# Graph attention with residual norm: pass sums weighted by shares from GpSimd, mask units kept in pairs, moments and normalising spread

## What is computed

```python
xt  = einsum('ni,hio->hno', x, W)                    # 4 heads of 64
src = einsum('hnf,hf->hn', xt, a[:, :64]);  dst = einsum('hnf,hf->hn', xt, a[:, 64:])
e   = leaky_relu(src[:, :, None] + dst[:, None, :], 0.2)
e   = where(adj > 0, e, -inf)
h   = einsum('hij,hjf->hif', softmax(e, axis=2), xt)   # heads side by side: 256 columns
out = layernorm(x + h)                               # over the 256 columns, eps 1e-5
```

## Time and profile before

| | before |
|---|---|
| median of 3 runs | 2212.24 us (2212.24 to 2214.11) |
| profiled execution | 2213.66 us |
| its span | 2212.1 us |
| PE matmul busy | 2108.5 us, 95% |
| DVE busy | 2069.6 us, 94% |
| ACT busy | 2011.0 us, 91% |
| GpSimd busy | 89.6 us, 4% |
| chain that ended last | PE 51%, DVE 21%, ACT 10%, issue 9% |

### The profile page before, as it was taken

The page is one execution under the profiler, slowest core; times in us unless marked ns, Lnnn a source line. Parts: engine busy times, 40 slices in busy tenths (PEclk is TensorE's granted clock), DMA queues, the critical chain, the costliest instruction groups (busy, mean ns, idle before and its releaser), DMA issues.

```text
span 2212.1 us, 79064 instructions
## 1 busy us (share of the span) xinstructions
PE 2108.5 (95%) x34304; PEld 2056.8 (93%) x34304; DVE 2069.6 (94%) x2288; ACT 2011.0 (91%) x2053; POOL 89.6 (4%) x88
## 2 busy tenths in 40 slices
PE   8768999999999999999999999999999999999996
PEld 4658999999999999999999999999999999999996
DVE  3899999999999999999999999999999999997775
ACT  3466998999999999999999999999999999999995
POOL 0110000010000100010000100010000100000000
PEclk9989999999999999999999999999999999999998
DMA  9699777766766676666766676666766677532310
GB/s 315 223 349 380 266 246 246 238 213 212 250 213 217 208 248 206 216 212 214 249 212 212 208 231 224 216 211 212 250 212 216 203 233 239 164 83 84 96 46 20
DMA packets 236441, 469.64 MB, mean 212 GB/s; under 512 B 14704, under 2 KB 22896, under 8 KB 236080
## 3 DMA queue, kind: packets, MB, share of 16 engines
q1 hardware_dynamic: 231600, 447.53, 61.8%
q0 software_dynamic: 4352, 16.78, 2.1%
q10 hardware_dynamic: 128, 0.13, 0.0%
HBM read 438.83 MB, written 25.56 MB: 210 GB/s over the span
## 4 chain that ended last, share of the span: by engine, by line
PE 51%; DVE 21%; ACT 10%; issue 9%; DMA 1%; DVEq 1%; POOL 0%; ACTq 0%; SPq 0%; POOLq 0%
PE acc L835 48%; ACT big L433 9%; DVE big L623 7%; DVE big L630 6%; PE tp L801 3%; DVE nat L539 2%; DVE big L615 1%; DVE stats L676 1%; ACT big L477 1%; DVE AT L553 1%; DVE big L637 1%; DVE nat L537 1%; DMA raw<-in_adj_dram 0%; DMA v_parts<-big 0%; DVE big L645 0%
## 5 line engine op out<-in xcount | busy, mean ns | idle before, releaser
L433 ACT ACTIVATE big<-big,d_all 128x1024 int8<-128x1024 f32 x1792 | 1896.5, 1141 | 84.0 <-PE acc L835 84.0
L835 PE MATMUL acc<-big 128*128 128x130 f16 x32768 | 1911.8, 220 | 30.4 <-DVE big L637 28.8
L835 PEld LDWEIGHTS acc<-big 128*128 128x128 fp8e5 x32768 | 1888.2, 98 | 39.7 <-issue 37.2
L623 DVE SCALAR_TENSOR_TENSOR big<-big,AT 128x1024 uint32<-128x1024 uint32 x512 | 627.2, 1225 | 62.1 <-ACT big L433 60.6
L630 DVE SCALAR_TENSOR_TENSOR big<-AT,big 128x1024 uint32<-128x1024 uint32 x512 | 626.7, 1224 | 4.3
L801 PE MATMUL tp<-ident,nat 128*128 128x128 f32 x1024 | 158.5, 278 | 41.9 <-DVE nat L537 33.0
L615 DVE TENSOR_SCALAR big<-big,d_all 128x1024 uint8<-128x1024 f32 x256 | 193.2, 755 | 0.0
L537 DVE TENSOR_SCALAR nat<-raw 128x2048 fp8e4<-128x2048 int32 x128 | 176.3, 1380 | 3.8 <-DMA raw<-in_adj_dram 3.8
L539 DVE TENSOR_SCALAR nat<-raw 128x2048 uint8<-128x2048 int32 x128 | 178.1, 1391 | 0.0
L553 DVE SCALAR_TENSOR_TENSOR AT<-AT,tp 128x512 uint32<-128x512 uint32 x224 | 154.8, 691 | 1.5
L801 PEld LDWEIGHTS tp<-ident,nat 128*128 128x128 f32 x1024 | 108.9, 142 | 49.2 <-DVE nat L537 38.8
(11 more groups left out here) (50 smaller groups left out, 377.9 us busy)
## 6 DMA issues: line engine op xcount, KB each, us to landing
raw<-in_adj_dram SPq DMA_DIRECT2D x256, 1024.0 KB, 5.7
big<-v_parts SPq DMA_DIRECT2D x512, 260.0 KB, 3.7
v_parts<-big SPq DMA_DIRECT2D x16, 1040.0 KB, 5.2
big<-s_rows SPq DMA_DIRECT2D x32, 512.0 KB, 5.5
AT<-in_x_dram SPq DMA_DIRECT2D x16, 512.0 KB, 6.5
big<-in_x_dram POOLq DMA_DIRECT2D x8, 1024.0 KB, 7.5
out_dram<-big POOLq DMA_DIRECT2D x8, 1024.0 KB, 9.0
big<-in_L_gnn_W_dram SPq DMA_DIRECT2D x2, 128.0 KB, 2.5
```

What stands on the lines that cost most here:

```text
L433: return nc.scalar.activation(sgn[:, g % NB, b, :], srow[:, h % 2, :], ACT.Sign, bias=dflat[:, r:r + 1], scale=-1.0)
L623: nc.vector.scalar_tensor_tensor(out=word(sgn, g % NB), in0=word(sgn, g % NB), scalar=EDGE[plane], in1=edges(g), op0=ALU.bitwise_and, op1= ...
L835: return nc.tensor.matmul(acc[:, k, o:o + 2 * VO], m[:, g % NB, b, t * P:(t + 1) * P], Vr[:, v:v + 2 * VO], start=opens, stop=False, skip_ ...
```

## The change

- **Shares.** GpSimd takes the two denominators of `u` times `ab` (`wden`, 128x16), adds them (`den`), and after DVE's reciprocal (`inverse`, after group 4) multiplies `ab` by it (`share`, 128x16). DVE multiplies `u` without its last column by `share` (`weigh`, after group 6) and adds both halves to `y` directly (`add_pos` after group 8, `add_neg` after group 9). `join` and `divide` go. For the last pass all of it is on DVE.
- **Pairs.** In steady chunks two units are kept by one instruction of 128x1024 (`keep_pair`) in steps 4j+3; it waits for the transposes of both, the second of which PE does at step 4j+2. `tp` is addressed as one tile of two banks, each unit's blocks in every second place. While chunk 0 runs, its own units are still kept alone, chunk 1's in pairs at steps 16+3j+2.
- **Moments and normalising.** Moments of tiles 0 to 2 after groups 10, 12, 14 of head 0, tiles 3 to 7 after groups 10 to 14 of head 1, `spread` after group 15 of head 1. ACT normalises tiles 0 to 5 in groups 5, 9, 13 of heads 2 and 3 and tiles 6 and 7 in groups 5 and 9 of the next chunk's head 0; in the last chunk, all 8 of the chunk before in groups 3, 7, 11, 15 of heads 2 and 3.
- GpSimd's program is unrolled, and ACT's loop starts one chunk later.

```diff
--- before.py
+++ after.py
...
@@ -248,13 +255,18 @@
         SIGNS_WITH = {9: 0, 11: 1, 13: 2, 15: 3}
-        def kept_at(first, after_first, s):
+        def kept_alone(first, s):
+            return made_at(True, s - 2) if first and 2 <= s < NG + 2 else []
+        def kept_pair(first, s):
             if first:
-                return [k for z in range(max(0, s - 2), s - 1) for k in made_at(True, z)]
-            if s < 3:
-                return [k - UN for z in range(s + 4 * NG - (2 if after_first else 3), s + 4 * NG - (1 if after_first else 2))
-                        if z < 4 * NG for k in made_at(after_first, z)]
-            return made_at(False, s - 3)
+                return [(s - NG) // 3] if s >= NG and (s - NG) % 3 == 2 else []
+            return [s // 4] if s % 4 == 3 else []
+        def sums4():
+            return u.rearrange("p (t c) v -> p t c v", c=2)
         @block.sync
...
@@ -380,19 +392,33 @@
             load_res(0, 0)
             load_res(1, 1)
-            def chunk(c, n):
-                deviation(c)
-                store(c, n)
-                pool.wait_ge(out_done, 16 * c + 16)
-                load_res(c + 2, n)
-            with pool.Fori(0, NC // 2 - 1) as i:
-                chunk(2 * i, 0)
-                chunk(2 * i + 1, 1)
-            for c in (NC - 2, NC - 1):
-                deviation(c)
-                store(c, c % 2)
+            def shares(p):
+                w = ab[:, p // H * T:(p // H + 1) * T, p % H, :]
+                pool.wait_ge(u_done, 3 * p + 6)
+                nc.gpsimd.tensor_tensor(out=wden[:, :, :], in0=sums4()[:, :, :, O], in1=w, op=ALU.mult).then_inc(wden_done, 1)
+                pool.wait_ge(wden_done, p + 1)
+                nc.gpsimd.tensor_tensor(out=den[:, :], in0=wden[:, :, 0], in1=wden[:, :, 1], op=ALU.add).then_inc(den_done, 1)
+                pool.wait_ge(rden_done, p + 1)
+                nc.gpsimd.tensor_tensor(out=share[:, :, :], in0=w, in1=rden[:, :].unsqueeze(2).broadcast_to([P, T, 2]),
+                                        op=ALU.mult).then_inc(share_done, 1)
+            for c in range(NC):
+                if c:
+                    shares(c * H - 1)
+                if c > 1:
+                    store(c - 2, c % 2)
+                    pool.wait_ge(out_done, 16 * (c - 1))
+                    load_res(c, c % 2)
+                shares(c * H)
+                if c:
+                    deviation(c - 1)
+                shares(c * H + 1)
+                shares(c * H + 2)
+            store(NC - 2, (NC - 2) % 2)
+            deviation(NC - 1)
+            store(NC - 1, (NC - 1) % 2)
             pool.wait_ge(out_done, 16 * NC)
...
                                          scale=rstd[:, t:t + 1]).then_inc(norm_done, 1)
-            def chunk(c, n, first=False):
+            def normalised_at(h, g, last):
+                if last:
+                    return [h % 2 * 4 + g // 4] if h >= 2 and g % 4 == 3 else []
+                return [(h - 2) * 3 + g // 4 - 1] if h >= 2 and g in (5, 9, 13) else []
+            def chunk(c, n, first=False, second=False, last=False):
                 for h in range(H):
                     p = c * H + h
                     act.wait_ge(row_in[h % 2], 32 * c + 16 * (h // 2 + 1))
...
@@ -489,14 +522,18 @@
                                 ins.then_inc(sgn_done, 1)
                             if g == 2 and b < 3 and not (first and h == 0):
                                 low(p - 1, b)
-                        if h == 1 and g >= 8 and not first:
-                            normalise(c - 1, 1 - n, (g - 8,))
+                        if h == 0 and g in (5, 9) and not first and not second:
+                            normalise(c - 2, n, (6 + g // 8,))
+                        if not first:
+                            normalise(c - 1, 1 - n, normalised_at(h, g, last))
             chunk(0, 0, first=True)
-            with act.Fori(0, NC // 2 - 1) as i:
+            chunk(1, 1, second=True)
+            with act.Fori(1, NC // 2 - 1) as i:
+                chunk(2 * i, 0)
                 chunk(2 * i + 1, 1)
-                chunk(2 * i + 2, 0)
-            chunk(NC - 1, 1)
+            chunk(NC - 2, 0)
+            chunk(NC - 1, 1, last=True)
             for part in range(3):
                 low(NP - 1, part)
             normalise(NC - 1, (NC - 1) % 2, range(T))
...
@@ -538,20 +575,21 @@
                 else:
                     nc.vector.tensor_scalar(to, of, 0.0, 59.0, ALU.is_gt, ALU.add).then_inc(conv_done, 1)
-            def keep(k, u, plane, fresh=False, n=0, g=0):
+            def keep(k):
                 dve.wait_ge(tp_done, k + 3)
-                if not fresh:
-                    z = (g - u // 2) % NG
-                    dve.wait_ge(pos_done if z == 0 else neg_done, n + 1 if z == 0 else n - z + 5)
-                to = AT[:, u // 2, :, u % 2, :]
-                of = tp[:, u % 2, :].bitcast(u32).rearrange("p (b i) -> p b i", b=B)
-                if fresh:
-                    nc.vector.tensor_scalar(to, of, EDGE[0], None, ALU.bitwise_and).then_inc(at_done, 1)
-                else:
-                    nc.vector.scalar_tensor_tensor(out=to, in0=to, scalar=EDGE[1 - plane], in1=of,
-                                                   op0=ALU.bitwise_and, op1=ALU.bitwise_or).then_inc(at_done, 1)
+                nc.vector.tensor_scalar(AT[:, k // 2, :, k % 2, :], tp[:, k % 2, :].bitcast(u32).rearrange("p (b i) -> p b i", b=B),
+                                        EDGE[0], None, ALU.bitwise_and).then_inc(at_done, 1)
+            def keep_pair(k, j, plane, n, g):
+                dve.wait_ge(tp_done, k + 4)
+                z = (g - j) % NG
+                dve.wait_ge(pos_done if z == 0 else neg_done, n + 1 if z == 0 else n - z + 5)
+                nc.vector.scalar_tensor_tensor(out=edges(j), in0=edges(j), scalar=EDGE[plane], in1=pair.bitcast(u32),
+                                               op0=ALU.bitwise_and, op1=ALU.bitwise_or).then_inc(at_done, 2)
             for g in range(NG):
                 dve.wait_ge(thin_done, g + 1)
...
@@ -637,38 +675,29 @@
                     ins = nc.vector.tensor_tensor(out=u_piece(piece), in0=u_piece(piece), in1=acc_piece(piece, 0), op=ALU.add)
                 ins.then_inc(u_done, 1)
-            def weigh(p, ec, eh):
-                dve.wait_ge(u_done, 3 * p + 6)
-                w = ab[:, bass.ds(ec * T, T), eh, :]
-                u4 = u.rearrange("p (t c) v -> p t c v", c=2)
-                nc.vector.tensor_tensor(out=u4, in0=u4, in1=w.unsqueeze(3).broadcast_to([P, T, 2, VO]),
+            def inverse(p):
+                dve.wait_ge(den_done, p + 1)
+                nc.vector.reciprocal(rden[:, :], den[:, :]).then_inc(rden_done, 1)
+            def weigh(p):
+                dve.wait_ge(share_done, p + 1)
+                u4 = sums4()[:, :, :, 0:O]
+                nc.vector.tensor_tensor(out=u4, in0=u4, in1=share[:, :, :].unsqueeze(3).broadcast_to([P, T, 2, O]),
                                         op=ALU.mult).then_inc(wu_done, 1)
-            def join(p):
+            def add_pos(p, ec, eh, n):
+                dve.wait_ge(res_in[n], 8 * (ec - n) + 16)
                 dve.wait_ge(wu_done, p + 1)
-                u4 = u.rearrange("p (t c) v -> p t c v", c=2)
-                nc.vector.tensor_tensor(out=u4[:, :, 0], in0=u4[:, :, 0], in1=u4[:, :, 1], op=ALU.add).then_inc(join_done, 1)
-            def inverse(p):
-                dve.wait_ge(join_done, p + 1)
-                nc.vector.reciprocal(rden[:, :], u.rearrange("p (t c) v -> p t c v", c=2)[:, :, 0, O]).then_inc(rden_done, 1)
-            def divide(p):
-                dve.wait_ge(rden_done, p + 1)
-                u4 = u.rearrange("p (t c) v -> p t c v", c=2)
-                nc.vector.tensor_tensor(out=u4[:, :, 1, 0:O], in0=u4[:, :, 0, 0:O],
-                                        in1=rden[:, :].unsqueeze(2).broadcast_to([P, T, O]), op=ALU.mult).then_inc(tr_done, 1)
-            def add_on(p, ec, eh, n):
-                dve.wait_ge(res_in[n], 8 * (ec - n) + 16)
-                dve.wait_ge(tr_done, p + 1)
-                u4 = u.rearrange("p (t c) v -> p t c v", c=2)
                 yh = y[n][:, :, eh * O:(eh + 1) * O]
-                nc.vector.tensor_tensor(out=yh, in0=yh, in1=u4[:, :, 1, 0:O], op=ALU.add).then_inc(added, 1)
+                nc.vector.tensor_tensor(out=yh, in0=yh, in1=sums4()[:, :, 0, 0:O], op=ALU.add).then_inc(half_added, 1)
+            def add_neg(p, eh, n):
+                dve.wait_ge(half_added, p + 1)
+                yh = y[n][:, :, eh * O:(eh + 1) * O]
+                nc.vector.tensor_tensor(out=yh, in0=yh, in1=sums4()[:, :, 1, 0:O], op=ALU.add).then_inc(added, 1)
             def moments(c, n, ts):
                 dve.wait_ge(added, 4 * c + 5)
...
@@ -699,13 +728,11 @@
                         if g < NG - 1:
                             if scalar_blocks(g + 1) < B:
                                 compares(n + 1, g + 1, h)
```

(62 more changed lines are left out.)

27 lines of the change are left out of this document (18 added, 9 removed).

## The result

The changed kernel took 2221.09 us, median of 6 runs (2219.28 to 2222.51), the kernel before 2212.14 (2211.19 to 2214.11): 1.0034 times as long, with an interval of 1.0023 to 1.0044. It is slower: the medians are 9.0 us apart, and the ratio with its interval stands for 5 to 10 us. The profiled execution took 2219.43, its span is 2217.6, against 2213.66 and 2212.1; of the changed kernel it is a quick one, 1.7 under the median, of the kernel before a slow one, 1.5 over it, so the two profiles differ by 5.8 only.

A forecast was written before the change was run, and what follows sets the result against it. PE bounds each pass, and DVE's reading of the sums delays it at boundaries. On the profiled 2213.66 us, +6.3 (steady chunks) +0.35 (loop's turn) -2.9 (chunk 0) -0.7 (last chunk) -0.1 (end) gave 2216.6, stated as 2216, range 2208 to 2226.

The forecast's parts named there:

- The cap of the pairs: Steady chunks: the pair waits for PE's transposes, limiting DVE's lead; each of the four boundaries costs 0.95 us.
- What is late in head 1: Boundary 1 to 2: five moments leave DVE 0.8 us late and spread adds 0.55; +0.6 for this transition.
- Bare waits at 0.23: DVE in groups 5, 9 and 13: rest masks wait for the masks right ahead of them, 0.23 us each.
- GpSimd hidden: GpSimd's three small operations a pass hold nobody; price taken as 0, between 0 and 0.25 us each.
- The division pays only where DVE is the bound: DVE loses 0.6 us a pass by the new division, a gain only in chunk 0, where DVE is the bound.
- The pairs in chunk 0: Chunk 0, heads 1 to 3: pairs replacing single units save DVE time, within a total of -2.9 us, ends -6 and 0.
- the cap bites: Chunk 0: the bad end of its forecast, the pairs' limit on DVE's lead acting there too, priced at 0.
- The last chunk: ACT is late there; the new order has six normalisings paid for eight, -0.9 us.
- a stall at the chunk's start: Start of the last chunk: the new boundary stall costs +0.2 us.
- The loop's turn: DVE stands 3.36 us there, before partly absorbed by its lead, now wholly on the boundary; +0.35 us.

The follow-up runs named there:

- e1: The kernel before with units kept in pairs and nothing else of the change; 2224.86 us, ratio 1.0053.
- e3: The changed kernel, pairs kept, with a pair's second unit converted and transposed one group earlier in steady chunks; 2201.41 us, ratio 0.9943.
- e6: The changed kernel with three short DVE steps moved between masks and rest masks in groups 5, 9 and 13; 2216.65 us, ratio 1.0014.
- e5: The changed kernel with two of GpSimd's three small operations done twice in every pass but the last; 2221.46 us, ratio 1.0035.
- e4: The kernel before with the shares and direct additions, normalising as before, moments after groups 10 and 11, spread after 12; 2209.45 us, ratio 0.9983.
- e9: The changed kernel with the units made while chunk 0 runs kept one by one, pairs from chunk 1 on; 2216.34 us, ratio 1.0018.
- e2: The changed kernel with its units kept one by one as before; 2194.57 us, ratio 0.9914.
- e7: The changed kernel without pairs, moments, spread and normalising moved off boundary 1 to 2, group 1's unit kept after parts 1 and 2 are read; 2185.89 us, ratio 0.9875.
- e10: The changed kernel with the last chunk's eight normalisings all in head 2's odd groups; 2224.96 us, ratio 1.0054.

## Why the prediction was right and where it was wrong

The time lay in the range, and the kernel is on the slower side, which the forecast had as likely as no difference. Point by point:

- **The cap of the pairs: right, in mechanism and size.** Pair at T+0.70 (forecast T+0.65), `high` at T+8.43 (8.25, and 0.12 for this boundary), part 1 1.60 later (1.60). All four boundaries stall; the table of T to T agrees within 0.2 at each, and a chunk is 252.7 (252.7). e1 shows it alone, e3 takes it away with the pairs left in.
- **What is late in head 1: right.** Boundary 1 to 2 is the worst, `high` at T+9.53 (9.6). Here DVE, not the pair's wait, is late, and the rows show why:

```profile
1568.80 0.61 PE L842 MATMUL tp<-ident,nat 128*128 128x128 f32 x4
...
1570.21 1.23 DVE L591 SCALAR_TENSOR_TENSOR AT<-AT,tp 128x1024 uint32<-128x1024 uint32 x1
1571.34 1.23 DVE L668 SCALAR_TENSOR_TENSOR big<-AT,big 128x1024 uint32<-128x1024 uint32 x1
1572.48 0.65 DVE L711 BATCH_NORM_AGGREGATE mv<-stats 128x2 f32<-128x6 f32 x8
...
1578.33 0.57 DVE L675 TENSOR_TENSOR big<-big,acc 128x390 f32<-128x390 f32 x1
```

  The pair starts at T+1.41, 0.76 late from five moments (0.8 forecast), and `spread` stands between it and `high` for 0.55 (0.55).
- **Bare waits at 0.23: right** (1.37 against 1.13; e6). **GpSimd hidden: right** (e5).
- **The division pays only where DVE is the bound: right for chunk 0, open for the rest.** e4 and e9 both show 0.6 a pass in chunk 0. A steady chunk of e4 gained nothing in sum, but there its later moments took back what the conversion in time gave. Its expectation had put a gain into the steady chunks, against the prediction's own step; that missed.
- **The pairs in chunk 0: wrong, and the largest error, 4.5 us.** The forecast took fewer instructions as the gain, -2.9 with 0 as the bad end, and it came out at +1.6, outside these ends. Of it the division is -1.9 (e9 against before: 65.18, 64.91 and 66.16 against 65.82, 65.52 and 66.78), as forecast. The pairs are +3.5 where -1.1 stood. The step that failed is the lower bound: "the cap bites" was priced at the loss of the gain, not as a wait on the bounding engine. Where DVE is the bound, each time it stands is paid in full.
- **The last chunk: right in kind, a little under-sized.** Kernels whose clock stayed up there compare cleanly: e4, with normalising as before, took 59.30, 63.23, 59.49 and 57.56; e9, with the change's, 59.33, 59.30, 61.26 and 57.57. Of these 2.1 less, 1.0 is the later start of the first `high`, which held nobody; from the last T to the end e9 took 268.19 and e4 269.35, 1.2 less, where 0.8 was forecast. Eight in head 1 cost 3.9, four in head 2 1.8, four in head 3 nothing. The two of head 0 are paid, as forecast: e2 starts the chunk as early as e4 and has them, and its head 0 took 60.28 against 59.30, 1.0 more. PE of e4, then of e2, up to its start of head 1:

```profile
1937.50 72.70 PE L855 MATMUL acc<-big 128*128 128x130 f16 x1266
```

```profile
1924.36 65.79 PE L869 MATMUL acc<-big 128*128 128x130 f16 x1152
1991.11 58.63 PE L869 MATMUL acc<-big 128*128 128x130 f16 x1024 [0.96 <-DVE big L675]
```

  e7, with four there, took 61.26. Six paid at 2.75 for eight at 3.93 is -1.2, where -0.9 was forecast; the +0.2 for a stall at the chunk's start didn't show.
- **The loop's turn: not there in this profile, more in others.** +0.35 was forecast; from T to T the pass with the turn took 65.56 after against 65.49 before, +0.1 where the other passes of its kind have +0.3. But e5, e6, e9 and e10 have the same order of DVE and PE at the turn and took 66.69, 66.76, 68.23 and 68.11. In these four PE's clock fell there, which the last section shows; the forecast has no term for it.

The profiled runs differ by 5.8, their spans by 5.5, and in that a -1.4 lies in the lead-in, whose code is the same and whose end scatters from 237.8 to 239.9 over the kernels here. Without it the difference is 7.0, within the interval of the runs. Against +2.95, then, the missing 4.0 are chunk 0 (4.5), less the last chunk and the end (0.4); the steady part, cut at the last T, is within 0.1. So the time lay in the range and the mechanism of the steady part was right, but the rise was more than twice the forecast one, by chunk 0. The medians are another 2 apart. Part of that may be the clock, which didn't fall at the turn in the changed kernel's profiled run; whether it fell in the other runs is not shown (their mean clock was 0.988 to 0.990, the profiled one's 0.991).

## What to carry to other kernels

When two small steps are joined into one, look first at what the joined step waits for: it takes the latest of their inputs, and on an in-order engine everything behind it, up to the work that another engine needs, moves with it. Count the distance from the producer to the joined step, in the producer's own groups; here the same pair cost 26 us with its second transpose one group ahead, and 7 with it two groups ahead, half of that in chunk 0, where nothing had been moved. Instructions saved count only where their engine is the bound, and a wait added there counts in full, so price a step separately in each stage, with a loss as one of the ends.
